# A delta-rule layer with two feed-forward halves: four call lists laid out anew, and GpSimd's scaled keys in halves of 256 columns

## What is computed

```python
x = x + 0.5 * ffn(layernorm(x))          # Hadamard transform, silu(gate) * up, Hadamard, down
x = x + mkda(layernorm(x))               # below; 16 heads, 4 keys and 4 values a token
x = x + 0.5 * ffn(layernorm(x))
# mkda, for every head, chunk by chunk, with a state S of 128 x 128:
q, k, v = (silu(short_conv(h @ W.T)) for W in (Wq, Wk, Wv))      # q and k are l2-normed
M    = tril(k exp(G - G') w, -1)                                   # w = beta * k, G sums log alpha
u    = solve_triangular(M, v - (k exp(G)) @ S, unit_diagonal=True)
o    = SCALE * (q exp(G) @ S + tril(q exp(G - G') w) @ u)
S    = exp(G_last) * S + (w exp(G_last - G)).T @ u
out  = (o * rstd * onorm_w * sigmoid(gate)) @ Wo.T
```

## Time and profile before

| | |
|---|---|
| median of 3 runs | 4942.76 us (4940.17 to 4954.71) |
| the profiled execution's own time | 4954.81 us |
| its span, first to last instruction | 4952.9 us |
| PE, DVE, ACT, POOL busy, share of the span | 91%, 84%, 69%, 65% |
| granted TensorE clock, mean | 0.98 |

### The profile page before, as it was taken

The page is one execution under the profiler, slowest core; times in us unless marked ns, Lnnn a source line. Parts: engine busy times, 40 slices in busy tenths (PEclk is TensorE's granted clock), DMA queues, the critical chain, the costliest instruction groups (busy, mean ns, idle before and its releaser), DMA issues.

```text
span 4952.9 us, 151365 instructions
## 1 busy us (share of the span) xinstructions
PE 4487.4 (91%) x63200; PEld 3133.3 (63%) x63200; DVE 4148.3 (84%) x7262; ACT 3394.4 (69%) x6708; POOL 3198.9 (65%) x5316
## 2 busy tenths in 40 slices
PE   8869999999999999999999999999999999999888
PEld 5536666666666666666666666666666666666655
DVE  3279999989999999999989999899999899999622
ACT  3267777777777777777777777777777777777531
POOL 0047777776777777777767777677777777677600
PEclk9989999999999999999999999999999999999799
DMA  2200000000000000000100000000000000000100
GB/s 87 88 26 24 26 25 25 15 24 25 34 32 18 25 25 26 25 15 24 34 32 30 15 24 26 25 25 14 30 30 25 25 14 25 26 25 9 37 9 22
DMA packets 49723, 135.45 MB, mean 27 GB/s; under 512 B 7056, under 2 KB 28176, under 8 KB 48400
## 3 DMA queue, kind: packets, MB, share of 16 engines
q1 hardware_dynamic: 49040, 125.77, 7.2%
HBM read 111.60 MB, written 14.16 MB: 25 GB/s over the span
## 4 chain that ended last, share of the span: by engine, by line
PE 57%; DVE 27%; ACT 8%; issue 6%; POOL 1%; DMA 0%; DVEq 0%; SPq 0%; ACTq 0%
PE bank L835 48%; DVE acc L1556 8%; PE bank L302 7%; DVE X L1553 7%; DVE sp_t L1553 2%; ACT o L1182 2%; PE bank L906 2%; DVE o L1556 2%; DVE Rs L1556 2%; DVE Pd L1661 1%; ACT L1471 1%; DVE Zc L1740 1%; DVE x1m L1553 1%; ACT Ztf L1181 1%; ACT rn L1182 1%
## 5 line engine op out<-in xcount | busy, mean ns | idle before, releaser
L1556 DVE SCALAR_TENSOR_TENSOR acc<-bank,vc,acc 128x510 f32<-128x510 f32 (+2 forms) x1728 | 1271.6, 739 | 124.5 <-ACT acc L1181 98.9
L2001 POOL TENSOR_TENSOR LZ<-LZ,LT 128x120 f32<-128x120 f32 (+26 forms) x1984 | 935.0, 471 | 155.5
L1553 DVE TENSOR_TENSOR X<-KQ,Fl 128x640 f32<-128x640 f32 x1024 | 1019.3, 1011 | 0.6 <-ACT Fl L1182 0.6
L1998 POOL TENSOR_TENSOR LT<-LA,LZ 128x120 f32<-128x120 f32 (+26 forms) x1984 | 921.0, 464 | 145.8
L1971 POOL COPY X<-KQ 128x640 f32<-128x640 f32 x256 | 249.2, 973 | 874.8 <-DVE KQ L1553 279.2
L835 PE MATMUL bank<-X 128*32 128x60 f32 (+1 forms) x32768 | 653.3, 206 | 136.2 <-DVE Pd L1661 85.9
L835 PEld LDWEIGHTS bank<-X 128*32 128x32 f32 x32768 | 527.3, 112 | 363.3 <-issue 205.6
L1181 ACT ACTIVATE Us<-bank 128x128 f32<-128x128 f32 x1024 | 282.4, 277 | 641.2 <-PE bank L835 630.2
L835 PE MATMUL bank<-xnTm,WK 128*128 128x512 f32 x1280 | 638.2, 623 | 42.1 <-DVE acc L1556 36.4
L1950 POOL TENSOR_TENSOR kdec<-KQ,Fe 128x512 f32<-128x512 f32 x256 | 337.4, 1318 | 303.8 <-PE bank L906 303.8
L835 PE MATMUL bank<-Rs,Ztf 128*128 128x128 f32 x2048 | 469.5, 315 | 68.1 <-DVE Rs L1556 48.0
(11 more groups left out here) (144 smaller groups left out, 9267.3 us busy)
## 6 DMA issues: line engine op xcount, KB each, us to landing
WK<-in_wkq SPq DMA_DIRECT2D x64, 704.0 KB, 6.0
WV<-in_wv SPq DMA_DIRECT2D x64, 576.0 KB, 3.8
WO<-in_wo SPq DMA_DIRECT2D x64, 128.0 KB, 2.0
wuh<-in_wu SPq DMA_DIRECT2D x2, 1024.0 KB, 7.4
xt<-in_x SPq DMA_DIRECT2D x4, 512.0 KB, 6.3
wuh_d<-wuh SPq DMA_DIRECT2D x1, 2048.0 KB, 6.3
x_d<-x SPq DMA_DIRECT2D x4, 512.0 KB, 3.0
xnT_d<-xT SPq DMA_DIRECT2D x4, 512.0 KB, 2.7
```

The source lines that it names most:

```text
L1553: return e.tensor_tensor(o, a, b, op)
L1556: return e.scalar_tensor_tensor(out=o, in0=a, scalar=sc, in1=b, op0=op0, op1=op1)
L1998: e.tensor_tensor(tmp, LA[:, j + 1:32, 8 * (j % R) + j // R].unsqueeze(2).broadcast_to([P, rr, cc]), LZ[:, j, 0:cc].unsqueeze(1).broadcast ...
L2001: e.tensor_tensor(LZ[:, j + 1:32, 0:cc], LZ[:, j + 1:32, 0:cc], tmp, SUB).then_inc(g_row, 1)
```

## The change

Nothing is computed otherwise. The bodies of the four lists hold the same calls as before in another order; two VectorE calls cross the end of the loop body (`conv_k(p+1, 1, 1)` now closes a round, `levels(p-1, 0, 1)` now stands in the next one). The turns of the two banks follow: `norm` and `vturn` 3 change places. In GpSimd's `spread`, each product of 128x512 is issued as two of 128x256, and the semaphore is raised by the second. `spread(p-1, 0, 0)` moves ahead of `level(p-1, 2)`, `level(p-1, 1)` moves behind `rows(p-2, 16)`.

```diff
@@ bank_use @@
-            ("vturn", 2, 2, a_vt, 4, 2), ("turn", 0, 1, a_kdT, 4, 0), ("norm", 0, 0, v_max, 1, 0),
-            ("vturn", 3, 2, a_vt, 4, 3), ("turn", 1, 1, a_kdT, 4, 1), ("k", 0, -1, v_ck, 15, 2),
+            ("vturn", 2, 2, a_vt, 4, 2), ("turn", 0, 1, a_kdT, 4, 0), ("vturn", 3, 2, a_vt, 4, 3),
+            ("norm", 0, 0, v_max, 1, 0), ("turn", 1, 1, a_kdT, 4, 1), ("k", 0, -1, v_ck, 15, 2),
@@ delta_tensor @@
                 rhs(p - 3, 0, 3)
-                products(p - 1, 0, 1)
+                update(p - 3, 1, 2)
                 solve(p - 3, 0, 3)
...
                 spare(p - 3, 10)
+                products(p - 1, 0, 1)
+                rhs(p - 3, 1, 4)
...
                 solve(p - 3, 0, 5)
+                products(p - 1, 0, 2)
                 products(p - 1, 0, 3)
...
                 project_v(p - 1, 1)
+                rhs(p - 3, 1, 7)
                 solve(p - 3, 0, 7)
-                rhs(p - 3, 1, 7)
+                solve(p - 3, 1, 7)
+                update(p - 3, 0, 7)
+                spare(p - 3, 22)
                 project_k(p, 3)
-                solve(p - 3, 1, 7)
-                spare(p - 3, 22)
-                update(p - 3, 0, 7)
                 update(p - 3, 1, 7)
                 spare(p - 3, 23)
-                mean_square(p - 3)
-                project_k(p, 4)
                 products(p - 1, 1, 0)
                 products(p - 1, 1, 1)
+                mean_square(p - 3)
                 products(p - 1, 1, 2)
+                project_k(p, 4)
+                output(p - 3, 0)
                 products(p - 1, 1, 3)
                 products(p - 1, 1, 4)
-                output(p - 3, 0)
                 output(p - 3, 1)
                 gate(p - 1)
                 turn_v(p - 2, 0)
                 project_v(p - 1, 2)
+                project_v(p - 1, 3)
                 products(p - 1, 2, 0)
+                first(p - 2, 0)
                 products(p - 1, 2, 1)
-                project_v(p - 1, 3)
-                first(p - 2, 0)
                 spare(p - 2, 30)
                 products(p - 1, 2, 2)
                 second(p - 2, 0)
                 spare(p - 2, 31)
                 products(p - 1, 2, 3)
+                products(p - 1, 2, 4)
                 turn_v(p - 2, 1)
-                products(p - 1, 2, 4)
                 third(p - 2, 0)
...
+                turn_v(p - 2, 3)
                 total(p)
-                turn_v(p - 2, 3)
                 products(p - 1, 3, 0)
+                products(p - 1, 3, 1)
+                spare(p - 2, 34)
+                products(p - 1, 3, 2)
                 first(p - 2, 1)
-                spare(p - 2, 34)
-                products(p - 1, 3, 1)
                 turn(p - 1, 1)
+                spare(p - 2, 35)
+                products(p - 1, 3, 3)
+                products(p - 1, 3, 4)
                 second(p - 2, 1)
-                spare(p - 2, 35)
-                products(p - 1, 3, 2)
-                products(p - 1, 3, 3)
+                project_k(p + 1, 0)
                 solve(p - 2, 0, 0)
-                products(p - 1, 3, 4)
-                project_k(p + 1, 0)
                 third(p - 2, 1)
                 spare(p - 2, 36)
                 update(p - 2, 0, 0)
+                fourth(p - 2, 1)
+                rhs(p - 2, 0, 1)
+                spare(p - 2, 37)
                 project_k(p + 1, 1)
-                fourth(p - 2, 1)
-                spare(p - 2, 37)
-                rhs(p - 2, 0, 1)
                 solve(p - 2, 1, 0)
...
@@ delta_scalar @@
                 spare(p - 3, 22)
                 tap_k(p, 3)
+                keep(p - 1, 0)
                 out_square(p - 3)
                 e.preload_act_table_set("natural_log_exp_and_others")
-                decay(p, 2)
-                spare(p - 3, 22)
                 spare(p - 3, 23)
                 out_root(p - 3, 0)
                 out_root(p - 3, 1)
-                keep(p - 1, 0)
+                decay(p, 2)
...
+                update(p - 2, 0, 0)
+                length(p - 1, 0)
                 factors(p, 0)
-                length(p - 1, 0)
-                spare(p - 2, 36)
-                update(p - 2, 0, 0)
+                spare(p - 2, 37)
+                fourth(p - 2, 1)
                 keep(p - 1, 3)
...
@@ delta_vector @@
-                distance(p, 1)
+                spare(p - 2, 35)
                 evacuate(p - 1, 3, 0)
                 evacuate(p - 1, 3, 1)
                 evacuate(p - 1, 3, 2)
                 evacuate(p - 1, 3, 3)
+                distance(p, 1)
                 take(p - 1)
...
@@ delta_gpsimd @@
-                    scaled(kdec[:, :, :], Fe[:, 1, :]).then_inc(g_kdec, 1)
+                    for hf in range(2):
+                        ins = scaled(kdec[:, 2 * hf:2 * hf + 2, :], Fe[:, 1, :], hf)
+                    ins.then_inc(g_kdec, 1)
                 else:
                     w.wait_ge(p_o, every(s - 2, 16))
-                    scaled(kexp[:, s % 2, 4 * q:4 * q + 4], Fe[:, 0, :]).then_inc(g_kexp, 1)
+                    for hf in range(2):
+                        u = 4 * q + 2 * hf
+                        ins = scaled(kexp[:, s % 2, u:u + 2], Fe[:, 0, :], hf)
+                    ins.then_inc(g_kexp, 1)
...
-                level(p - 1, 1)
                 rows(p - 2, 12)
                 rows(p - 2, 16)
+                level(p - 1, 1)
                 rows(p - 2, 20)
                 rows(p - 2, 24)
                 rows(p - 2, 28)
+                spread(p - 1, 0, 0)
                 level(p - 1, 2)
                 level(p - 1, 3)
-                spread(p - 1, 0, 0)
```

More of the change, by code:

```diff
@@ L1046, in delta_tensor @@
                 rhs(p - 3, 0, 3)
-                products(p - 1, 0, 1)
+                update(p - 3, 1, 2)
                 solve(p - 3, 0, 3)
-                update(p - 3, 1, 2)
+                turn(p - 2, 3)
                 spare(p - 3, 8)
-                turn(p - 2, 3)
-                update(p - 3, 0, 3)
                 rhs(p - 3, 1, 3)
                 project_k(p, 2)
+                update(p - 3, 0, 3)
+                solve(p - 3, 1, 3)
                 rhs(p - 3, 0, 4)
-                solve(p - 3, 1, 3)
+                update(p - 3, 1, 3)
                 spare(p - 3, 10)
+                products(p - 1, 0, 1)
+                rhs(p - 3, 1, 4)
+                spare(p - 3, 11)
                 solve(p - 3, 0, 4)
-                update(p - 3, 1, 3)
-                spare(p - 3, 11)
+                project_v(p - 1, 0)
+                solve(p - 3, 1, 4)
                 update(p - 3, 0, 4)
[L1062 to L1065, removed]
+                update(p - 3, 1, 4)
                 spare(p - 3, 13)
                 rhs(p - 3, 0, 5)
-                update(p - 3, 1, 4)
+                rhs(p - 3, 1, 5)
                 spare(p - 3, 14)
                 solve(p - 3, 0, 5)
+                products(p - 1, 0, 2)
                 products(p - 1, 0, 3)
-                rhs(p - 3, 1, 5)
                 update(p - 3, 0, 5)
@@ L1152, in delta_tensor @@
                 spare(p - 2, 2)
+                turn(p - 1, 2)
+                rhs(p - 2, 1, 1)
                 update(p - 2, 0, 1)
-                rhs(p - 2, 1, 1)
-                turn(p - 1, 2)
+                solve(p - 2, 1, 1)
                 rhs(p - 2, 0, 2)
-                solve(p - 2, 1, 1)
                 spare(p - 2, 4)
-                update(p - 2, 1, 1)
+                products(p, 0, 0)
                 spare(p - 2, 5)
                 solve(p - 2, 0, 2)
+                update(p - 2, 1, 1)
                 rhs(p - 2, 1, 2)
                 update(p - 2, 0, 2)
-                products(p, 0, 0)
+                spare(p - 2, 7)
                 solve(p - 2, 1, 2)
-                spare(p - 2, 7)
         def delta_scalar(e, ffn):
@@ L1805, in delta_vector @@
             for p in range(-1, NS + 3):
-                conv_k(p, 1, 1)
-                spare(p - 3, 7)
                 rhs(p - 3, 0, 3)
                 conv_k(p, 1, 0)
-                levels(p - 1, 0, 2)
                 update(p - 3, 1, 2)
                 distance(p - 1, 4)
+                levels(p - 1, 0, 1)
                 spare(p - 3, 8)
+                levels(p - 1, 0, 2)
+                rhs(p - 3, 1, 3)
                 update(p - 3, 0, 3)
+                distance(p - 1, 5)
+                update(p - 3, 1, 3)
@@ L1815, in delta_vector @@
+                rhs(p - 3, 0, 4)
                 levels(p - 1, 0, 3)
-                rhs(p - 3, 1, 3)
-                diagonal(p - 2)
-                rhs(p - 3, 0, 4)
+                spare(p - 3, 10)
+                rhs(p - 3, 1, 4)
+                spare(p - 3, 11)
                 conv_k(p, 2, 2)
-                spare(p - 3, 10)
-                update(p - 3, 1, 3)
-                distance(p - 1, 5)
-                spare(p - 3, 11)
-                rhs(p - 3, 1, 4)
                 conv_k(p, 2, 1)
+                levels(p - 1, 0, 4)
@@ L1826, in delta_vector @@
```

(23 more changed lines are left out.)

161 lines of the change are left out of this document (77 added, 84 removed).

## The result

| | before | after |
|---|---|---|
| median | 4948.74 us (4 runs, 4940.17 to 4957.55) | 5028.35 us (4 runs, 5012.72 to 5034.63) |
| ratio | | 1.0156, 95% interval 1.0124 to 1.0188 |
| the profiled execution, its span | 4952.9 us | 5026.2 us |
| granted TensorE clock, mean | 0.98 | 0.95 |

The change makes the kernel 1.6% slower. The forecast was 4821 us with a range that ended at 4950, so it missed in sign and in range. Among the kernels timed further down, layout_alone and before_long_row each had one run at a much lower clock (15535.58 us at 0.505, 5402.66 us at 0.818), and their medians are those of the other three runs. The first two views answer to the earlier trace rows: the steady part, then two rounds that follow each other, then three stretches inside the second; and the calls of `take`. The columns are those of the earlier trace rows.

What follows compares the result with a forecast made beforehand. It took one chain a round as the bound: TensorE 43.3 us, way out 4.0, VectorE 20.8. Terms -1.43 + 0 - 0.3 - 0.2 = -1.93 us x 63 = -122 us gave 4821 us, range 4750 to 4950.

Steps and rivals of the forecast that it cites:

- the part on moves: Other calls moved between places in the lists, project_v(3) among them, SP's queue untouched: terms 0.
- Instructions run out: Rival, 10%: 208 small records in a row in quarter 2 cost one 1.4 us wait a round; 4911 us.
- no change: Rival, 9%: waits only move; new waits of way out and recurrence take what VectorE gives; 4943 us.
- The sum: All terms together: -1.93 us a round, x 63 = -122 us; forecast 4821 us, given 57%.
- The halves: GpSimd's products split in two shorten VectorE's stands before quarter 2's last evacuate: -1.43 us a round.
- The way out: TensorE after the recurrence, up to output: new waits 0.9, 0.6, 0.15 us replace old 1.51; term 0.
- The recurrence: rhs, solve and update get other neighbours, changing waits for Rs and Us: -0.3 us a round, between -1.1 and +0.6.
- The tile sizes: TensorE's lists have 34 tile-size changes a round instead of 37, at 0.07 us each: -0.2 us.
- The way out decides: Rival, 14%: halves win nothing, VectorE stays the bound, later keep and evacuate(1,0) add 1.1 us a round; 5013 us.

Runs made afterwards that it cites:

- layout_alone: The changed lists with GpSimd's products whole as before the change: 5023.78 us, ratio 1.0153 to the kernel before.
- before_long_row: The kernel before with one TensorE call moved, project_v(p-1, 3) ahead of products(2, 0): 5104.19 us, ratio 1.0316 to the kernel before.
- row_broken: The changed kernel with project_v(p-1, 3) moved back behind products(2, 1), first(p-2, 0) still behind it: 4771.48 us, ratio 0.9631 to the kernel before.
- both_mended: row_broken plus the two SyncE lines of loads_late: 4746.88 us, ratio 0.9598 to the kernel before.
- idle_full: both_mended with TensorE made to wait for a later WV load in the recurrence every fourth round: 4869.18 us, ratio 0.9842 to the kernel before.
- keep_first: both_mended with ScalarE's keep(p-1, 0) ahead of tap_k(3) again: 4792.24 us, ratio 0.9686 to the kernel before.
- way_out: both_mended with out_square ahead of keep(0), gated ahead of levels(1, 4), mean_square ahead of products(1, 0), project_k(4) ahead of products(1, 2): 4814.62 us.
- mended_whole: both_mended with GpSimd's products whole again: 4749.82 us, ratio 0.9601 to the kernel before.
- loads_late: The changed kernel with SyncE's loads of WV and WK held until project_k(p+1, 1), in the recurrence: 4821.98 us, ratio 0.9731 to the kernel before.

## Why the prediction was wrong

**The step that failed** is in the part on moves: "`project_v(3)`" was followed to GpSimd's `level(3)` and no further, and "SP's queue is not touched. [...] Terms: 0." SyncE's list is indeed unchanged, but its loads of WV and WK wait for the end of `project_v(3)`. Moving that call moved 1280 KB of transfers to the head of a row of 208 small records. before_long_row has this step alone and loses 155 us; row_broken undoes it alone and wins 257. In its place the runs showed waits for instructions (over 0.7 us: 32 us in all before, 139 after) and TensorE at half clock for some 500 us instead of some 200.

**The rival that came true was priced by half.** "Instructions run out" named the row, the sign (the waits without releaser double) and one wait of 1.4 us a round; it did not name the loads. Its own evidence was partly another thing: the 0.29 us wait at 2085 is one of the 58 of its length that have no packet behind them. The added waits are 84.4/63 = 1.3 us a round net, and 1.7 if only waits over 0.7 us are counted (139 - 32 = 107 us). What the price lacked is the clock. As the clock has only the levels 1 and 0.5 here, a mean of c is a share of 2(1 - c) of the span at half clock: 2 x 0.05 x 5026 = 503 us here, 2 x 0.02 x 4953 = 198 before, 2 x 0.013 x 4750 = 123 in both_mended. By an estimate from idle_full a microsecond at half clock costs about 0.41 us: 122 - 56 = 66 us more, for 2 x 0.029 x 4875 - 123 = 160 us at half clock. Against both_mended that gives 380 x 0.41 = 156 us of clock and 127 us of waits (all without releaser, those of the transposes too: 151.9 against 24.8), 283 us, where the two spans differ by 276.6. Other waits differ between the two kernels as well (for `Ztf` 25.4 against 8.6), so the sum is an account to within some 20 us and not a proof. With the half clock added (305 us over the kernel before, x 0.41 = 125) this rival would have stood at 4911 + 125 = 5036 and not at 4911, on the other side of no change; that uses a clock that only the result showed.

**The sum came out in size, and partly by luck.** An undisturbed round takes 65.5 to 66.2 us against the 66.17 worked out, and both_mended, which is the change without its fault, has 65.88. But the terms that gave it did not hold one by one:

- *The halves, -1.43.* Wrong in this setting. They win 1.0 us a round in the old lists and 0 in the new. The reading behind it held (the engines take turns; `softplus` goes from 1656 ns to 689 on the mean), but the new order had won that already. A half takes 0.80 us (`kdec`) and 0.75 (`kexp`) on the mean, not 0.68, so a pair costs more than one whole product (1.36 and 1.32 in layout_alone).
- *The way out, 0.* The three new waits came where and nearly as long as said, 2.01 us against the old 1.51: a loss of 0.5. What was wrong is to add them up as separate terms. keep_first and way_out show one chain through VectorE and the table load; a wait taken away in front comes back behind.
- *The recurrence, -0.3.* Too small. The waits for `Rs` fell from 48.0 to 29.3 us, 0.3 a round, and those for `Us` from 24.0 to 1.1, another 0.36. That is 0.66 in all, more than twice the term, and the new wait for `Us` that it expected at `update(1,2)` did not come.
- *The tile sizes, -0.2.* Not measured apart. In mended_whole the lists alone are 2.2 us below the 68.1 of before; 1.4 of it is the `Pd` wait of quarter 3, which is gone there without the halves. Which moves did that was not tried.
- *The way out decides (slower, 14%).* The sign came true and the reason did not. Its condition held, that the halves win nothing, but VectorE was not left as the bound: row_broken has the same way out and is 3.7% faster than before.

What stays open: why waits for instructions of up to 2.1 us come at a row of 208 with the loads moved away (loads_late). A packet is behind these too (38 of the 39 over 0.7 us), and they get fewer as the row gets shorter (55.5 us with 208 records, 20.3 with 144), but nothing here shows how far ahead of TensorE the packets are asked for. That the loads hold the packets back is read from when the packets start and from what moving the loads does; no run holds back a packet by itself.

## What to carry to other kernels

Before a call is moved, follow who waits for its end, the transfer queue first: a load starts with its last reader, and it can start where the instruction stream is at its densest. Rows of hundreds of small products want a long instruction between them, and no large load beside them. Price a wait of TensorE of 3 to 4 us at twice its length (3.5 us cost 7.6 here), because the clock can fall with it.

## What the runs showed of the hardware

- Packets of 16 KB on a queue of kind "instruction" move beside the data (498 of them, 8.16 MB), and 55 of TensorE's 56 waits without releaser over 0.7 us end 1.2 to 1.6 us after one of them. With 1280 KB of loads at the head of a row of 208 small records such a wait reached 4.7 us; with the loads in the recurrence (loads_late), 2.1.
- Sixteen waits of 3.1 to 4.1 us with full-tile products next to them each came with 3.4 to 13.7 us at 1.2 GHz, although TensorE was then busy almost without a pause.
- Shorter waits can do it too: in way_out a wait of 0.99 us and one of 0.80 close behind it came with 3.4 us at 1.2 GHz in 17 of 63 rounds.
- The rows read as VectorE and GpSimd taking turns by whole instructions. In the kernel before `softplus` took 1.70 us on the mean in the 61 rounds in which its record overlaps `kdec` or `kexp` (1.3 and 1.5 us on the mean) and 0.68 in the other 3; with halves in the same lists it took 1.17 in 60 rounds and 0.68 in 4.
- The cost is not a matter of the number of small products: both kernels have the same 63200 records on TensorE. Where they and the loads stand is worth 281 us, 5.6% (4746.88 against 5028.35 us, with two calls moved in TensorE's list and two lines added to SyncE's).
